# Output projection of the last two batches in plain float32, and the last two V products next to each other

## What is computed

```
xn = layernorm(x)
mixed = xn @ Wqkv.T                       # per head: q, k, v
attn = softmax(q @ k.T / 4)               # per sequence and head, 256 x 256
ctx = attn @ v                            # 256 x 16 per head
s = ctx_of_all_heads @ Wproj.T + bproj
h = gelu(xn @ proj1.T + proj1_bias)
g = silu(h @ proj2.T + proj2_bias)
return x + s * g
```

## Time and profile before

| what | value |
|---|---|
| median of the three timed runs | 131.39 us (131.06 to 132.0) |
| the profiled execution: its own time / its span | 131.83 us / 129.9 us |
| mean granted TensorE clock | 0.991 |
| PE busy | 120.5 us (93%) |
| PEld (weight loads, beside PE) | 94.3 us (73%) |
| DVE busy | 87.7 us (68%) |
| ACT busy | 73.3 us (56%) |
| POOL busy | 52.0 us (40%) |
| transfers | 13.29 MB |

### The profile page before, as it was taken

How to read it: one execution, slowest core, us unless ns; L and a number is a source line. 1 busy time by engine, 2 the same in 40 slices (tenths; PEclk the granted TensorE clock), 3 DMA queues, 4 the chain that set the end, 5 groups by cost and what they waited for, 6 DMA issues and landing times.

```text
span 129.9 us, 2686 instructions
## 1 busy us (share of the span) xinstructions
PE 120.5 (93%) x1008; PEld 94.3 (73%) x1008; DVE 87.7 (68%) x179; ACT 73.3 (56%) x108; POOL 52.0 (40%) x59
## 2 busy tenths in 40 slices
PE   6899999999998999999998999999798999999960
PEld 5697998888897989986776788756665767656540
DVE  0787992500004899999996899741935758499983
ACT  4162894699970101027749405797869678968310
POOL 3246494099996000007465650069651101433100
PEclk9999999999999999999999999999999999999996
DMA  4999589999999999800000000810000010010203
GB/s 132 322 386 395 156 184 151 160 168 170 157 174 177 147 178 171 122 20 3 0 0 0 4 11 13 287 38 10 0 10 0 8 40 27 21 42 1 86 0 121
DMA packets 7553, 13.29 MB, mean 102 GB/s; under 512 B 1012, under 2 KB 2676, under 8 KB 7284
## 3 DMA queue, kind: packets, MB, share of 16 engines
q1 hardware_dynamic: 7540, 13.11, 46.2%
HBM read 5.51 MB, written 1.05 MB: 50 GB/s over the span
## 4 chain that ended last, share of the span: by engine, by line
PE 56%; DMA 16%; DVE 12%; issue 6%; ACT 5%; SPq 3%; POOL 1%; DVEq 0%; ACTq 0%
PE bank L650 31%; DMA ks<-stage 12%; PE bank L774 10%; PE bank L746 7%; PE bank L726 6%; DVE negm L566 5%; DMA wqkv_raw<-wqkv 3%; ACT PT L479 2%; SPq L309 2%; PE bank L683 1%; DVE cd L583 1%; ACT hG L459 1%; DVE veps L508 1%; DVE ctxn L590 1%; DVE fin L625 1%
## 5 line engine op out<-in xcount | busy, mean ns | idle before, releaser
L566 DVE TENSOR_REDUCE negm<-bank 128x4 f32<-128x1024 f32 x32 | 37.0, 1217 | 16.8 <-PE bank L726 16.7
L371 POOL TENSOR_TENSOR hTl<-hG,hTh 128x512 fp32r<-128x512 f32 x16 | 20.3, 1298 | 24.0 <-ACT hTh L463 24.0
L479 ACT ACTIVATE PT<-bank 128x1024 f32<-128x1024 f32 x22 | 21.1, 1025 | 5.2 <-PE bank L746 5.1
L650 PE MATMUL bank<-w2h,hTh 128*128 128x256 f32 x64 | 14.3, 305 | 0.9 <-DVE mm L570 0.7
L485 ACT ACTIVATE th<-yh 128x256 f32<-128x256 f32 x8 | 3.3, 418 | 20.5 <-DVE yh L608 20.4
L746 PE MATMUL bank<-qs,ks 50*128 50x256 f32 x128 | 13.1, 312 | 1.2 <-ACT PT L479 0.9
L459 ACT ACTIVATE hG<-bank,b1s 128x512 f32<-128x512 f32 x16 | 10.9, 680 | 5.1 <-PE bank L650 5.1
L383 POOL TENSOR_TENSOR bg<-gate,bps 128x256 f32<-128x256 f32 x8 | 6.0, 748 | 19.0 <-DVE gate L522 10.0
L746 PEld LDWEIGHTS bank<-qs,ks 50*128 50x128 f32 x128 | 8.9, 185 | 6.0 <-ACT PT L479 2.1
L650 PE MATMUL bank<-w2h,hTl 128*128 128x256 f32 x64 | 12.9, 282 | 0.0
L650 PE MATMUL bank<-w2l,hTh 128*128 128x256 f32 x64 | 12.8, 282 | 0.0
(11 more groups left out here) (79 smaller groups left out, 219.9 us busy)
## 6 DMA issues: line engine op xcount, KB each, us to landing
qs<-stage SPq DMA_DIRECT2D x12, 256.0 KB, 11.1
ks<-stage SPq DMA_DIRECT2D x12, 256.0 KB, 17.8
w_raw<-w SPq DMA_DIRECT2D x2, 1024.0 KB, 8.6
xs<-x SPq DMA_DIRECT2D x4, 256.0 KB, 4.1
xb<-x SPq DMA_DIRECT2D x1, 1024.0 KB, 5.4
out<-fin SPq DMA_DIRECT2D x8, 128.0 KB, 1.7
wqkv_raw<-wqkv SPq DMA_DIRECT2D x3, 256.0 KB, 5.0
wps<-wp SPq DMA_DIRECT2D x8, 32.0 KB, 6.8
```

The source lines that it names most:

```text
L371: nc.gpsimd.tensor_tensor(hTl[:, n % FC, :], hG[:, n % FC, :], hTh[:, n % FC, :].bitcast(f32), ALU.subtract).then_inc(h_lo, 1)
L479: nc.scalar.activation(exp_of(w), scores_of(*s), ACT.Exp).then_inc(exp_done, 1)
L566: nc.vector.tensor_reduce(negm[:, j, :, :, s[1] % 2, b].rearrange("p q a -> p a q"), scores_of(*s), axis=AX.X, op=ALU.max, negate=True).th ...
L650: m = nc.tensor.matmul(dst, lhs(kc, a), rhs(kc, b), start=first and n == 0, stop=last and n == len(todo) - 1)
```

## The change

The tiles of output batches 2 and 3 are no longer split. TensorE multiplies the turned context itself, in float32, with the unsplit weights `wps`: one float32 matmul for each half of a tile where there were three of float32r. The four `TURN` steps of these batches are gone: three copies on POOL, one on ACT and four subtractions on DVE. The chunks of batch 3 are turned into a buffer of their own, `ctxT_last`, so that they wait for no reader of batch 2. The end of the list is written in a new order: `PV 15` directly after `PV 14`, then all of the projections from tile 5 on; `FIN 4` now stands behind `PV 14`.

```diff
-        if d >= 2:
+        if 2 <= d < 6:
             order.append(("TURN", d % 2, d // 2 - 1))
...
-    order += [("ST", 28), ("ST", 29), ("PJ", 3, 0), ("PJ", 3, 1), ("TURN", 1, 2), ("FIN", 3), ("PV", 13),
-              ("ST", 30), ("ST", 31), ("PJ", 4, 0), ("PJ", 4, 1), ("FIN", 4), ("PV", 14), ("TURN", 0, 3), ("PJ", 5, 0),
-              ("PV", 15), ("PJ", 5, 1)]
-    return order + [("PJ", 6, 0), ("PJ", 7, 0), ("TURN", 1, 3), ("FIN", 5), ("PJ", 6, 1), ("FIN", 6),
+    order += [("ST", 28), ("ST", 29), ("PJ", 3, 0), ("PJ", 3, 1), ("FIN", 3), ("PV", 13),
+              ("ST", 30), ("ST", 31), ("PJ", 4, 0), ("PJ", 4, 1), ("PV", 14), ("FIN", 4), ("PV", 15)]
+
+    return order + [("PJ", 5, 0), ("PJ", 5, 1), ("PJ", 6, 0), ("PJ", 7, 0), ("FIN", 5), ("PJ", 6, 1), ("FIN", 6),
                     ("PJ", 7, 1), ("FIN", 7)]
...
+        ctxT_last = at("ctxT_last", [P, KC, SQ], f32, xTl_at + 6 * KB)
...
+        def ctx_of(j):
+            return ctxT_last if j == HP // 2 - 1 else ctxT
...
-                        if j >= 1:
+                        if 1 <= j < HP // 2 - 1:
                             dve.wait_ge(ct_lo, KC * (j - 1) + kc + 1)
 
-                        nc.vector.transpose(ctxT[:, kc, :], ctxn[:, kc, :]).then_inc(turned, 1)
+                        nc.vector.transpose(ctx_of(j)[:, kc, :], ctxn[:, kc, :]).then_inc(turned, 1)
...
+                    if j >= 2:
+                        pe.wait_ge(turned, KC * j + kc + 1)
+                        last = nc.tensor.matmul(bank_of("PJ", u, 0)[:, 0:E], ctx_of(j)[:, kc, qt * P:(qt + 1) * P],
+                                                wps[:, kc, :], start=kc == 0, stop=kc == KC - 1)
+                    else:
+                        pe.wait_ge(ct_hi, KC * j + kc + 1)
+                        last = product(...)
```

More of the change, by code:

```diff
@@ L205, in layer_kernel @@
         pv_made, cd_out, rc_done, norm_done = (sem(n) for n in ("pv_made", "cd_out", "rc_done", "norm_done"))
-        turned, ct_hi, ct_last, ct_lo, wp_hi, wp_lo = (sem(n) for n in ("turned", "ct_hi", "ct_last", "ct_lo", "wp_hi", "wp_lo"))
+        turned, ct_hi, ct_lo, wp_hi, wp_lo = (sem(n) for n in ("turned", "ct_hi", "ct_lo", "wp_hi", "wp_lo"))
         f2_made, b2_half, yh_done, th_done, gate_done, bg_done, xb_done = (
@@ L264, in scores_of @@
             return bank[:, home[s][0]:home[s][0] + 2, :].rearrange("p a (q c) -> p a q c", q=2)
-        def high_of(kc, j):
-            return (ct_last, 1) if (kc, j) == (1, HP // 2 - 1) else (ct_hi, KC * j + kc + 1)
+        def ctx_of(j):
+            return ctxT_last if j == HP // 2 - 1 else ctxT
         block = ctx.enter_context(nc.Block())
@@ L390, in _ @@
                     kc, j = s[1:]
[L391 to L395, removed]
+                    pool.wait_ge(turned, KC * j + kc + 1)
+                    nc.gpsimd.tensor_copy(cTh[:, j % 2, kc, :], ctxT[:, kc, :]).then_inc(ct_hi, 1)
                 last = 4 if s == ("ST", 0) else s[1] if s[0] == "F2" and s[2] == 3 else TT if s[0] == "GATE" else 0
@@ L485, in _ @@
                     nc.scalar.activation(th[:, u % 2, :], yh[:, u % 2, :], ACT.Tanh).then_inc(th_done, 1)
[L486 to L491, removed]
         @block.vector
@@ L615, in _ @@
                     kc, j = s[1:]
-                    dve.wait_ge(*high_of(kc, j))
+                    dve.wait_ge(ct_hi, KC * j + kc + 1)
                     nc.vector.tensor_tensor(cTl[:, j % 2, kc, :], ctxT[:, kc, :],
@@ L779, in _ @@
                     j, qt = divmod(u, 2)
-                    pe.wait_ge(*high_of(kc, j))
                     if u == 0:
@@ L784, in _ @@
                         wait_free(s)
[L785 to L789, removed]
+                    if j >= 2:
[4 more added lines that the diff above has]
+                        pe.wait_ge(ct_hi, KC * j + kc + 1)
+                        last = product(bank_of("PJ", u, 0)[:, 0:E],
+                                       lambda k, a: (cTh, cTl)[a][:, j % 2, k, qt * P:(qt + 1) * P],
+                                       lambda k, a: (wph, wpl)[a][:, k, :], range(kc, kc + 1),
+                                       first=kc == 0, last=kc == KC - 1, lhs_lo=(ct_lo, KC * j + kc + 1),
+                                       passes=((0, 0), (0, 1), (1, 0)))
                     if kc == KC - 1:
```

## The result

The changed kernel took 135.07 us (median; 133.93 to 136.66 in four runs) where the kernel before took 131.35 (131.06 to 132.0, four runs). The ratio is 1.0247, with a 95% interval of 1.0159 to 1.0335: slower by 2.5%, where 0.5% faster was forecast. The profiled execution took 133.93 us with a span of 132.0, 2.10 more than before in both.

What follows compares the result with a forecast made beforehand. The prediction took PE's sequence to bound the kernel up to about 123 us, then a chain of latencies ending on DVE. Gains of 0.08 + 0.47 + 0.14 = 0.69 us turned 131.39 into 130.7, range 130.1 to 131.5.

Steps and rivals of the forecast that it cites:

- the last sentence of the sum: Whole kernel: 131.83 becomes 131.14, and on the scale of the timed runs 131.39 becomes 130.7, 0.5% less.
- The clock falls: Rival, chance 0.03: the clock falls already after the V products, slowing the last projections; 132.5 us.
- its terms: Last stage: 0.08 from DVE's transposition, 0.47 from ACT's step, 0.14 from the shorter last half; together 0.69 us.
- A float32 record each 0.217 us: Float32 projections on PE: records 0.217 us from start to start, taken from the warm-up matmuls.
- Tile 4's block: Projection of tile 4 in the chain: 1.05 us with four float32 records, 0.90 before; PV 14 starts 0.15 later.
- The V pair: PV 14 and PV 15 side by side on PE: 1.85 us together, 0.17 saved.
- DVE's transposition of group 15: On DVE behind PV 14: starts at 123.06 instead of 123.14, 0.08 us gained, held up by DVE's order.
- PE's idle time ahead of its last four records: PE behind the eight projection records: free at 124.40, 0.19 us before the turned chunk at 124.59.
- From the turn to PE: Last turned chunk: PE reads it 0.48 us after the turn starts; ACT's copy and hand-over, 0.47, leave the path.
- The last half of tile 6: Last projections on PE: two float32 records take 0.71 us where three matmuls took 0.85.
- The weight loads show: Rival, 0.14 in whole or part: float32 weight loads aren't hidden, stride 0.33, PE becomes the bound; 131.9 us.
- DVE doesn't hold up group 15: Rival, chance 0.12: its transposition starts when the product is ready; gain 0.88 or near 1.1, 130.5 to 130.3 us.

Runs made afterwards that it cites:

- e4_base_a: The kernel before, unchanged, first of two copies run as kernels of their own beside two copies of the changed kernel; 135.44 us median of 6.
- e1_again: The changed kernel run again without any edit, against the kernel before; 132.5 us median of 12, ratio 0.9964.
- e1_order: The kernel before with only the order changed, PV 14 and PV 15 next to each other, split kept; 133.89 us median of 12, ratio 1.0005.
- e3_again: The changed kernel run a third time without any edit, against the kernel before; 134.88 us median of 6, ratio 1.0155.

## Why the prediction was wrong

**The forecast of the time failed** (130.7, range 130.1 to 131.5, measured 135.07); only 0.03 stood on slower. The step that failed is the last sentence of the sum: that 131.39 minus the gain would be the new time. It took for granted that everything ahead of the stage stays as it was, a term put at nothing without a reason, and took the spread of three runs for what the kernel's time can do. In its place the runs showed a wait for `ks` of 0.5 to 5.3 us, from execution to execution and in both kernels, with a slow stretch of matmuls behind the long ones: in the profiled pair it put the stage 2.81 us later and so buried a gain of 0.71. The page of the profile had the warning: its chain of waits gives 16% of the span to DMA, 12% to `ks<-stage` alone. I read only the end of the chain and opened with "TensorE carries it nearly without a break", which the chain bears out for the last stage and not for the whole: PE has 56% of it, and ahead of 40 us the last 16 us are one transfer. No rival named a wait outside the stage. The range should have held the landing of a saturated stream of transfers that PE was already waiting for.

**"The clock falls"** was a rival with 0.03, for the wrong place. It fell at about 43 us, behind a wait on transfers (granted 0.55 from 43 to 44 us and 0.50 from 44 to 46, where PE had resumed at 41.89), not at the projections.

**The stage, point by point.** The sum was right, and its terms came out at 0.11 (0.08 forecast), 0.45 (0.47) and 0.14 (0.14):

- A float32 record each 0.217 us: four take 1.13 now, so (1.13 - 0.38 - 0.11) / 3 = 0.213, with the 0.11 of the first load that is seen. Tile 4's block is 1.06 in the chain (1.05 forecast).

```profile
122.39 1.13 PE L776 MATMUL bank<-wps,ctxT 128*128 128x256 f32 x4
123.45 1.06 PE L764 MATMUL bank<-PT_more,VA 128*17 128x256 f32 x16
124.33 1.05 PE L764 MATMUL bank<-PT,VA 128*17 128x256 f32 x16
125.30 1.13 PE L776 MATMUL bank<-wps,ctxT 128*128 128x256 f32 x4
```

- The V pair: 123.45 to 125.30 is 1.85, as forecast.
- DVE's transposition of group 15: 125.84, 4.05 behind the start of the stage, where it was 123.14 - 118.98 = 4.16. Gained 0.11 (0.08 forecast), and by the order that was named: the experiment with the addition moved back frees it.
- PE's idle time ahead of its last four records was about 0.1 instead of 0.2: the fifth of the eight records starts 0.97 behind the first (126.27 against 125.30) where 0.87 was reckoned.
- From the turn to PE 127.38 - 126.88 = 0.50 (0.48 forecast); ACT's step is gone.
- The last half of tile 6 is 0.71 (0.71 forecast); DVE's multiplication follows the start of the turn by 1.24 instead of 1.83.
- In all 0.71, against 0.69 (the rest is rounding and 0.01 in the turn).

**The other rivals.** "The weight loads show" did not happen: the stride is 0.213, not 0.33. The rule that spoke for it, in "TensorE: Matmul & The Clock Gate" of the Trainium skill, Part 3, "The mechanism", doesn't hold for these full-height loads of 190 ns. The stride agrees with what the page's Part 2 says of loads into a background buffer; that it is this buffer no run here shows. "DVE doesn't hold up group 15" did not happen in the changed kernel either: DVE's order held it up. Once `FIN 4` is moved back it does, and the whole gain is 8.72 - 7.67 = 1.05, where that rival had 0.88, or near 1.1 with faster records.

**What stays open.** Why the transfers run at 172 GB/s in one execution and at 143 in another, with equal packets, and why the landing moves even where the rate is much the same, wasn't found, nor why the first four pairs of runs split so cleanly. The moment of issue doesn't decide it: `e4_base_a` issued the transfer that landed last earlier than any other profile that shows it, at 23.29, and had it under way for 21.66 us; `e1_again` issued its own 0.46 later than the kernel before and saw it land 0.19 earlier. One thing in the data is odd: the reference runs of the kernel before were above 133 in 42 of 79 cases, its copies run as kernels of their own in 19 of 24 (on the same two chips the reference had 24 of 46). Something in how a kernel's runs are placed may favour the reference; no run here isolates it. The measured ratio of 1.0247 stands as measured, but it is not the cost of this edit.

## What to carry to other kernels

Before an edit of 0.5% is priced, look along the whole chain for a place where an engine waits a little on a saturated stream of transfers: such a wait can be long in the next execution, its scatter (here 6 us) buries the edit, and four close runs don't prove it absent. Measure the edit from a fixed point inside the trace, or cover the wait with idle work in both kernels and compare those. And taking out an instruction pays only if its place in the order stays empty: the addition put where a subtraction had stood cost 0.33 us of the possible gain.

## What the hardware showed

- The same transfers (7553 packets, 13.29 MB) ran at 143 to 172 GB/s between 30 and 40 us over the 17 profiles, with the 16 engines busy all along, and the landing that PE waits for moved from about 40.1 to 45.0 us over the 14 in which it shows. The two go together only roughly: `e1_order` waited 0.7 us at 152 GB/s, `e4_base_a` 5.3 us at 149.
- The granted clock behind the wait, as the table has it: 1.00 in the profiles in which PE had stood for 0.5 to 1.5 us, a mean of 0.66 to 0.83 over the stretch in those in which it had stood for 1.7 to 5.3. The two levels of the Trainium skill's "TensorE: Matmul & The Clock Gate", Part 1, are seen in the pace: eighteen matmuls in 2.35 us behind the short waits, 3.44 to 3.72 behind waits of 1.7 to 2.7, and 4.14 in `e3_again` and `e4_base_a`, where the mean clock of the stretch was lowest.
- A float32 matmul of 128 x 128 weights and 256 columns is two records, 0.213 to 0.217 us apart, with its loads of 190 ns hidden; against three float32r matmuls 0.12 apart it costs PE 0.07 us more, and it needs neither the copy nor the subtraction of a split.
